# A two-layer decoder on one core: expert products computed transposed, expert weights fetched per tile, first weights of each stage awaited apart, two stages' inputs fetched ahead

## The chip, the cores and the metric

The kernel runs on one core of a Trainium2 chip. A core has five engines that run side by side and meet at semaphores: TensorE (PE, with its weight loads shown as PEld), VectorE (DVE), ScalarE (ACT), GpSimd (POOL) and SyncE (SP), which in this kernel issues most DMAs. All DMAs share 16 DMA engines. The metric is the device time of one execution in microseconds (us), lower is better. The median of three runs of the kernel before is 3891.22 us (3890.78 to 3893.25).

## The reference

The input x has 8 batches of 512 rows of 256 values, float32. Six sublayers follow each other, each with a residual sum and a layer norm:

```python
x = _layernorm(x + _L0_attn_ref(x, ...))     # 16 heads, scores times a decay table
x = _layernorm(x + _L0_xattn_ref(x, ctx, ctx, mask))   # keys and values are 64 context rows
x = _layernorm(x + _L0_ffn_ref(x, ...))      # 256 -> 1024, butterflies, gelu, butterflies, -> 256
x = _layernorm(x + _L1_attn_ref(x, ...))     # 16 heads of 64, rotary, causal
x = _layernorm(x + _L1_xattn_ref(x, ctx, ...))   # 8 heads over 512 + 64 keys
x = _layernorm(x + _L1_ffn_ref(x, gamma, beta, router_w, W1, W2))
```

The last one is a mixture of 8 experts, of which each row takes its best two:

```python
logits = jnp.einsum('btd,ed->bte', xn, router_w)
probs = jax.nn.softmax(logits / TEMP, axis=-1)
w, idx = jax.lax.top_k(probs, K)                       # K = 2
h = jax.nn.silu(jnp.einsum('btd,edf->betf', xn, W1))   # W1: 8 x 256 x 1024
y = jnp.einsum('betf,efd->betd', h, W2)                # W2: 8 x 1024 x 256
out = jnp.einsum('bte,betd->btd', wdense, y)           # and out + res
```

## The kernel before

x stays on the chip all the time, in `x_all`, 32 tiles of 128 rows. The sublayers run one after the other. Each is a function that opens a block: a written program for each engine, with semaphore waits placed by hand. A block ends when all five engines have ended, and the next one starts with all of them. So whatever an engine waits for at the head of a block stands alone on the clock. The loops over batches are unrolled, and within a block the order of the work on each engine is the order of the text.

- `load_block` (L268) fetches the identity matrix and all 4 MB of x, and ends when both have landed.
- `attention` (L446) serves three sublayers by its `kind`: `a0`, `a1` and `x1`. At its head SP issues the list `loads` (L713 to 732), and PE, DVE and SP wait for all of it at once (`wait_ge(weights, 16 * len(loads))`, L784, L1206, L1220). PE then starts the first batch from the list `START`: transpose x (`xT`, L803), the latent product (`lat`, L813; not in x1), the first queries and keys (`item`), and, in a1 and x1, the first values (`v`). In a0 GpSimd also writes zeros to the 33 MB area `moe_sent`, four MB ahead of each batch (L1157 to 1162).
- `cross_attention_heads` (the x0 stage, L1417) fetches the context twice over (`ctxT`, `vnat`), the head mask and the mask, waits for all, lets DVE build the values and the bias, and only then splits the context into two parts (ACT L1577, DVE L1663). GpSimd needs both parts for the keys (L1621), PE needs the keys for the scores (L1553).
- `fold_butterflies` (L1731) multiplies the butterfly stages into one up and one down matrix. SP issues `w_con`, `high`, the placed stages of the up side (`lowup`, 3.5 MB in two DMAs), four small ones and the down side. PE runs `rounds(0)` over `lowup` (L1793), then L1803, then `rounds(1)` over `lowdown`. DVE first folds the high stages of the down side (L1864, L1868), then those of the up side (L1877), the latter in turns with ACT (L1843).
- `route` (L2070) picks the experts of the last two batches, places the rows in `moe_sent` sorted by expert (GpSimd's indirect DMAs, L442), and SP fetches the weights of all experts, `w1` and `w2`, 8 MB each, in 16 DMAs (L2124, L2125). GpSimd ends with a wait for the last row to land.
- `experts` (L2277) runs 72 tiles of 128 sorted rows. Which expert a tile has is read from `expert_of` into a register. For a tile PE transposes the rows (`experts_X`, L2353), multiplies them with `w1` in two halves of 512 columns (`experts_H`, L2373: the rows are the loaded weights, `w1` streams through), and ACT applies silu (`experts_h`, L2406). Then come eight transposes back (`experts_HT`, L2386), copied out by DVE (L2432), and the product with `w2` (`experts_Y`, L2361), copied out by DVE (L2423) and stored by SP. PE's order for tile i is H(i), Y(i-1), X(i+1), HT(i). SP fetches the rows of tile i+2 once X(i) is done. An fp32 product is shown as two PE instructions per call, a transpose as one.
- `combine` (L2436) gathers the two results of each row, sums and normalises.

Of the kernel before, what the change touches and what calls it, by code (L numbers as in the profile page):

```python
# [39 lines left out]
CLEAR = 8 * P  # L40

# [226 lines left out]
def load_block(nc, sh, x, ident):  # L268

    with ExitStack() as ctx:  # L270
        env = Env(nc, ctx, "load")
        loaded = env.sem("loaded")
        block = ctx.enter_context(nc.Block())

        @block.sync
        def _(sp):
            sp.dma_start(sh.ident[:], ident).then_inc(loaded, 16)
            sp.dma_start(sh.x_all[:, :, :], x.rearrange("b (q p) d -> p (b q) d", p=P)).then_inc(loaded, 16)
            sp.wait_ge(loaded, 32)
# [166 lines left out]
def attention(nc, sh, kind, w, ro):  # L446
# [118 lines left out]
    with ExitStack() as ctx:  # L565
# [77 lines left out]
        weights = sem("weights")  # L643
        ready = sem("ready")
# [68 lines left out]
        loads = [(wo[:], tiled(w["w_o"]))]  # L713
        if a0:
            loads += [(wq[:], w["w_q"].rearrange("(t p) g c -> p t g c", p=P)),
                      (wkT[:], tiled(w["w_kT"])), (wvT[:], tiled(w["w_vT"])), (wdn[:], tiled(w["w_down"])),
                      (wupk[:], w["w_up_k"]), (wupv[:], w["w_up_v"]), (table[:], w["decay"]),
                      (halves[:], w["halves"])]
        if a1:
            loads += [(wq[:], tiled(w["w_q"])), (wdn[:], tiled(w["w_down"])),  # L720
                      (wupk[:], w["w_up_k"]),
                      (wupv[:], w["w_up_v"]), (table[:], w["causal"]), (cos[:], w["cos"]), (sin[:], w["sin"])]
        if x1:
            loads += [(wq[:], tiled(w["w_q"])), (wk1[:], tiled(w["w_k1"])), (wv1[:], tiled(w["w_v1"])),
                      (wk2[:], tiled(w["w_k2"])), (wv2[:], tiled(w["w_v2"])), (bo[:], w["b_o"].to_broadcast([P, D]))]
            loads += ro.loads(w)
        N_READY = {"a0": 4, "a1": 1, "x1": 6}[kind]

        @block.sync
        def _(sp):  # L730
            for to, src in loads:
                sp.dma_start(to, src).then_inc(weights, 16)
            if x1:
                sp.dma_start(ctxT[:], tiled(w["ctxT"][0])).then_inc(ctx_in, 16)

            def swap_halves(b, n):

                wait_apart(sp, (weights, 16 * len(loads)), (raw_done, b * 4 * G + n + 1), (sin_done, b * 4 * G + n + 1))
                for k in range(4):
                    sp.dma_start(raw_swapped[32 * k:32 * k + 32, n % 2, :],  # L740
                                 raw[32 * (k ^ 1):32 * (k ^ 1) + 32, n % 4, :]).then_inc(swapped[n % 2], 16)

            def spread_rows(b, k):

                wait_apart(sp, (weights, 16 * len(loads)), (turned, b * G + (k + 2)))
                g = k % G
                sp.dma_start(inv_dram[g % 2], inv_rows[:, g % 2, :]).then_inc(spilled, 16)
                wait_apart(sp, (weights, 16 * len(loads)), (spilled, b * 16 * G + 16 * (k + 1)))
# [32 lines left out]
        def _(pe):  # L781
            pe.sem_inc(t_full, T_CREDIT)
            pe.sem_inc(pv, 2)
            pe.wait_ge(weights, 16 * len(loads))  # L784
            if a0:

                pe.wait_ge(ready, 2)
# [94 lines left out]
            def finish(seg, turn, b, work):  # L882

                qt = work[1]

# [150 lines left out]
            def begin():  # L1036
                for work in START:
                    run(start, 0, 0, work)
# [116 lines left out]
        def _(pool):  # L1155
# [8 lines left out]
            if x1:  # L1164
                pool.wait_ge(ready, N_READY)
                pool.wait_ge(ro.cleared, 16 * (SLOTS // CLEAR))
# [10 lines left out]
            if a1:  # L1177
                pool.sem_inc(sin_done, 2)
                pool.sem_inc(low, LOW_GROUP)
                pool.wait_ge(ready, N_READY)  # L1180
# [22 lines left out]
        def _(dve):  # L1203

            if a0:
                dve.wait_ge(weights, 16 * len(loads))  # L1206
                nc.vector.memset(inv[:], 1.0).then_inc(ready, 1)
                nc.vector.tensor_tensor(wkT[:], wkT[:], wvT[:], ALU.add).then_inc(ready, 1)
                nc.vector.memset(v_sb[:], 0.0).then_inc(ready, 1)
# [3 lines left out]
            else:  # L1213
# [6 lines left out]
                dve.wait_ge(weights, 16 * len(loads))  # L1220
                if x1:
                    nc.vector.memset(ro.ones[:], 1.0).then_inc(ready, 1)
                    nc.vector.tensor_scalar(ro.first[:], ro.iota[:, 0:NE], float(AREA), None, ALU.mult).then_inc(ready, 1)
                    nc.vector.tensor_scalar(ro.upto[:, 0, :], ro.iota[:, 0:NE], float(AREA), None,
                                            ALU.mult).then_inc(ready, 1)
# [70 lines left out]
            def step(seg, turn, b, s, prev, own, nxt):  # L1296
# [7 lines left out]
                route = x1 and own and b >= 2  # L1304
                if route and s == 0:
# [95 lines left out]
            def begin():  # L1401
                for work in START:
                    if work[0] == "item":
                        low_parts(start, 0, 0, work[1], work[2])

# [9 lines left out]
def cross_attention_heads(nc, sh, w):  # L1415
# [15 lines left out]
    with ExitStack() as ctx:  # L1431
# [3 lines left out]
        ctxT = sb("ctxT", [P, DT, B, SC])  # L1435
        ctx_hl = sb("ctxhl", [P, 2, DT, B * SC], F32R)
        keys = sb("keys", [P, 2, DT, B, HH, SC], F32R)
        v_nat = sb("vnat", [P, B, D])
        v_all = sb("v", [P, B, PR * 2 * VC])
        hmask = sb("hmask", [P, HH])  # L1440
        mask = sb("mask", [P, B * QT, SC], I32)
# [13 lines left out]
        loaded = sem("loaded")  # L1455
# [52 lines left out]
        LOADS = DT + 2 + 2  # L1508

        @block.sync  # L1510
        def _(sp):
            for t in range(DT):
# [1114 lines left out]
```

## Time and profile before

| | us |
|---|---|
| median of three runs | 3891.22 |
| the profiled execution, its own time | 3911.24 |
| span of its instructions | 3909.4 |
| PE busy in the span | 3308.2 (85%) |
| PEld busy | 2437.9 (62%) |
| DVE busy | 2117.3 (54%) |
| ACT busy | 1919.8 (49%) |
| POOL busy | 972.7 (25%) |

The span is cut into 40 slices of 97.7 us. In the page's second part a digit is the busy share of a slice in tenths, PEclk is the granted clock of TensorE in tenths of full speed, and the last two rows are the share of the 16 DMA engines and GB/s:

```profile
PE   5888888858689589998899968999999939999970
PEclk9999999978899799999999989999999969999985
DMA  3111111010200222222222220000000051111113
```

PE is the busiest engine nearly everywhere. The dips are the borders of the stages: the start, slice 8 (a0 to x0), slice 10 (x0 to the fold), slice 13 (a1), slice 23 (x1), slice 32 (the routing), and the last 120 us, `combine`, where PE has no work. Times in rows are microseconds from the start of the span; a row of the timeline gives the start, the duration, the engine, line and operation, what is written and read, the number of instructions merged in it, and in brackets the idle time ahead of it and what ended that.

### The profile page before, as it was taken

To read this page: it belongs to the slowest core of one execution; us is meant where nothing else is said; L and a number is where in the kernel's file an instruction comes from. 1 tells how busy PE (TensorE), PEld (TensorE's weight loads), DVE (VectorE), ACT (ScalarE), POOL (GpSimd) and SP (SyncE) were. 2 spreads that over 40 slices of the span, in tenths; PEclk is the share of its full clock that TensorE was granted. 3 is DMA by queue.
4 is the path that set the end of the run, shared out by engine and by line. 5 is a ranking of instruction groups with operands and counts; after the bars stand their busy time and mean duration, and the time that the engine had idled before them with its cause. 6 is when DMAs were issued, how large, how long until landed. Compare 5 with 4: busy or idle time off the path is not lost. (4 is left out here: it accounts for less than half of the span.)

```text
span 3909.4 us, 73528 instructions
## 1 busy us (share of the span) xinstructions
PE 3308.2 (85%) x25632; PEld 2437.9 (62%) x25632; DVE 2117.3 (54%) x6935; ACT 1919.8 (49%) x4678; POOL 972.7 (25%) x790
## 2 busy tenths in 40 slices
PE   5888888858689589998899968999999939999970
PEld 3666566548678356666666656777777727677750
DVE  4777777756667345554555543566666642222226
ACT  4887788734432265555655544655555501111110
POOL 0000000026200376766677620001111130000014
PEclk9999999978899799999999989999999969999985
DMA  3111111010200222222222220000000051111113
GB/s 110 52 50 61 40 70 66 26 31 1 101 1 1 64 57 51 58 50 55 53 58 50 52 60 22 13 13 23 24 24 24 25 214 34 34 33 33 34 43 111
DMA packets 111253, 187.53 MB, mean 48 GB/s; under 512 B 23792, under 2 KB 66224, under 8 KB 106032
## 3 DMA queue, kind: packets, MB, share of 16 engines
q1 hardware_dynamic: 100000, 131.44, 11.8%
q0 software_dynamic: 10896, 51.39, 3.5%
q8 instruction: 216, 3.54, 0.4%
q14 instruction: 141, 1.16, 0.1%
HBM read 91.93 MB, written 57.28 MB: 38 GB/s over the span
## 5 line engine op out<-in xcount | busy, mean ns | idle before, releaser
L955 PE MATMUL a_T<-ident,a_t 128*128 128x128 f32 x3328 | 500.7, 284 | 89.1 <-ACT a_pT L1119 62.6
L955 PEld LDWEIGHTS a_T<-ident,a_t 128*128 128x128 f32 x3328 | 376.1, 144 | 285.4 <-issue 249.5
L1119 ACT ACTIVATE a_pT<-a_T 128x512 f32<-128x512 f32 (+3 forms) x768 | 368.4, 511 | 223.2 <-PE a_T L955 223.1
L1354 DVE CUSTOM_DVE_ANT_0 a_t<-a_A,a_decay 128x512 f32<-128x512 f32 x512 | 323.0, 687 | 102.5 <-PE a_A L920 102.2
L1132 ACT ACTIVATE a_t<-a_t,a_neg 128x512 f32<-128x512 f32 x512 | 362.7, 716 | 6.1 <-DVE a_neg L1365 4.9
L1359 DVE CUSTOM_DVE_ANT_0 a_t<-a_A,a_table 128x384 f32<-128x384 f32 (+3 forms) x512 | 221.2, 487 | 179.8 <-PE a_A L932 178.8
L1189 POOL TENSOR_TENSOR a_rsin<-a_rawswapped,a_sin 128x512 f32<-128x512 f32 x128 | 170.5, 1332 | 529.0 <-DMA a_rawswapped<-a_raw 445.9
L1132 ACT ACTIVATE a_t<-a_t,a_mx 128x384 f32<-128x384 f32 (+3 forms) x512 | 280.0, 551 | 0.0
L2423 DVE COPY experts_y<-experts_Y 128x256 f32<-128x256 f32 x72 | 30.6, 425 | 438.6 <-PE experts_Y L2361 438.6
L2373 PE MATMUL experts_H<-ex_w,experts_xgT 128*128 x576 | 261.4, 597 | 0.8 <-ACT experts_xgT L2400 0.6
L2361 PE MATMUL experts_Y<-ex_w,experts_hT 128*128 x1152 | 260.5, 379 | 1.0 <-DVE experts_hT L2432 1.0
L2361 PEld LDWEIGHTS experts_Y<-ex_w,experts_hT 128*128 128x128 f32 x1152 | 218.8, 190 | 61.3 <-issue 35.2
L1119 ACT ACTIVATE x_pT<-x_T 128x512 f32<-128x512 f32 (+1 forms) x320 | 177.0, 592 | 138.4 <-PE x_T L955 118.0
L1359 DVE CUSTOM_DVE_ANT_0 x_t<-x_A,x_table,x_mx 128x512 f32<-128x512 f32 x256 | 177.2, 748 | 122.2 <-PE x_A L932 121.7
L2464 POOL DMA_INDIRECT combine_got<-moe_results,moe_fetch x64 | 62.1, 970 | 627.0 <-PEq L2442 593.6
L1328 DVE COPY a_pT<-a_T 128x512 f32<-128x512 f32 (+3 forms) x256 | 148.2, 579 | 126.6 <-PE a_T L955 125.8
L2406 ACT ACTIVATE experts_h<-experts_H 128x512 f32<-128x512 f32 x144 | 86.0, 597 | 240.8 <-PE experts_H L2373 240.8
L1132 ACT ACTIVATE x_t<-x_t,x_mx 128x576 f32<-128x576 f32 x256 | 194.7, 765 | 0.0
L891 PE MATMUL a_A<-a_wo,a_oT 128*128 128x256 f32 x640 | 165.2, 411 | 32.7 <-DVE a_mx L1359 12.9
L976 PEld LDWEIGHTS a_O<-a_pT,a_v 128*64 128x64 f32 x2560 | 139.0, 138 | 67.9 <-ACT a_pT L1119 38.2
L932 PE MATMUL a_A<-a_khl,a_qhl 64*128 64x128 f32 (+3 forms) x1536 | 157.2, 336 | 25.2 <-POOL a_khl L1199 22.4
L1162 POOL DMA_DIRECT2D moe_sent<-a_zeros x33 | 17.5, 539 | 642.0 <-ACT a_xT L1088 642.0
(337 smaller groups left out, 6901.5 us busy)
## 6 DMA issues: line engine op xcount, KB each, us to landing
moe_sent<-a_zeros POOLq DMA_DIRECT2D x33, 1024.0 KB, 8.0
a_rawswapped<-a_raw SPq DMA_DIRECT2D x512, 64.0 KB, 2.0
a_invrep<-a_inv_dram SPq DMA_DIRECT2D x64, 256.0 KB, 4.0
ex_w<-in_f_w_dram SPq DMA_DIRECT2D x16, 1024.0 KB
experts_xg<-moe_sent SPq DMA_DIRECT2D x72, 128.0 KB, 2.0
moe_results<-experts_y SPq DMA_DIRECT2D x72, 128.0 KB, 1.7
x_invrep<-x_inv_dram SPq DMA_DIRECT2D x32, 256.0 KB
x_all<-in_x_dram SPq DMA_DIRECT2D x1, 4096.0 KB, 14.5
```

Of the source, the lines that this page charges most:

```text
L891: mm = pe.matmul(bank[:, 0:D], oT[:, t, qt * P:(qt + 1) * P], wo[:, t, :], start=(t == 0), stop=(t == n_o - 1))
L932: mm = pe.matmul(A[seg.bank(at)][:, 0:keys(u)], q_hl[r, gp, ql, j // 2, q], k_hl[r, gp, kl_, j // 2, 0:keys(u)], start=(n == 0), stop=(n = ...
L955: mm = pe.transpose(bank[:, kt, :], t_of(u, j, kt * P, (kt + 1) * P), sh.ident[:])
L976: mm = pe.matmul(O[pr][64 * half:64 * half + 64, q], v_sb[:, kt, col], p_tile(u, j, kt), start=(kt == 0), stop=last, skip_group_check=True)
L1119: nc.scalar.activation(to, of, ACT.Copy).then_inc(t_empty, 1)
L1132: nc.scalar.activation(t_of(u_e % U, j, 0, n), t_of(u_e % U, j, 0, n), ACT.Exp, bias=neg[:, slot, j:j + 1], scale=SCALE if a0 else -1.0, a ...
L1189: nc.gpsimd.tensor_tensor(rsin[:], raw_swapped[:, n % 2, :], sin[:], ALU.mult).then_inc(sin_done, 1)
L1328: nc.vector.tensor_copy(p_tile(u, 3, 0, kts), bank[:, 0:kts, :] if kts > 1 else bank[:, 0, :])\
L1354: nc.vector.tensor_tensor_reduce(t_of(s, j, 0, n), A[seg.bank(name)][:, 0:n], table[:, at:at + n], 1.0, LOWEST, ALU.mult, ALU.max, mx[:, s ...
L1359: nc.vector.tensor_tensor_reduce(t_of(s, j, 0, n), A[seg.bank(name)][:, 0:n], table[:, at:at + n], -SCALE, mx1[:, slot, j:j + 1] if x1 els ...
L2361: mm = pe.matmul(Y[parity][:], hT[:, f, :], w2[:, bass.ds(e, 1), f, :].rearrange("p a d -> p (a d)"), start=(f == 0), stop=(f == FT - 1))
L2373: mm = pe.matmul(H[half][:], xgT[:, dt, :], w1[:, bass.ds(e, 1), dt, half * 512:(half + 1) * 512] .rearrange("p a f -> p (a f)"), start=(d ...
```

## The change

It has four parts.

1. Experts. The inner values come out transposed: for each 128 of the 1024 columns, that block of `w1` is the loaded operand and the transposed rows stream through. So the back transposes, their DVE copies and the tile `h` are gone. SP fetches the `w1` of each tile by itself, 1 MB into one of two buffers, once H of the tile two before is done. `w2` stays resident and is fetched in `route`. PE's order for tile i is now H(i), X(i+1), Y(i-1).

```diff
@@ experts, SP
+            def weights_of(i, parity):
+                e = sp.value_load(expert_of[0:1, i:i + 1], min_val=0, max_val=NE - 1)
+                sp.dma_start(w1[:, parity], w1_dram[bass.ds(e, 1)].rearrange("a (t p) f -> p (a t) f", p=P))\
+                  .then_inc(w1_in[parity], 16)
+            for i in range(2):
+                sp.dma_start(xg[:, i, :], tile_rows(sp, i)).then_inc(xg_in[i], 16)
+                weights_of(i, i)
 step:
+                if i + 2 < TILES:
+                    sp.wait_ge(xt_full, i + 1)
+                    sp.dma_start(xg[:, parity, :], tile_rows(sp, i + 2)).then_inc(xg_in[parity], 16)
+                    sp.wait_ge(h_full, i * 2 + 2)
+                    weights_of(i + 2, parity)
                 if not first:
                     store(i - 1, 1 - parity)
@@ experts, PE
                 pe.wait_ge(xt_done, i + 1)
-                pe.wait_ge(h_act, i * 2 + 2)
+                pe.wait_ge(w1_in[parity], pair * 16 + 16)
                 for half in range(2):
-                    for dt in range(DT):
-                        mm = pe.matmul(H[half][:], xgT[:, dt, :],
-                                       w1[:, bass.ds(e, 1), dt, half * 512:(half + 1) * 512]
-                                       .rearrange("p a f -> p (a f)"), start=(dt == 0), stop=(dt == DT - 1))
+                    if i:
+                        pe.wait_ge(h_act, i * 2 - 1 + half)
+                    for j in range(FT // 2):
+                        f = half * (FT // 2) + j
+                        for dt in range(DT):
+                            mm = pe.matmul(H[half][:, j, :], w1[:, parity, dt, f * P:(f + 1) * P], xgT[:, dt, :],
+                                           start=(dt == 0), stop=(dt == DT - 1))
                     mm.then_inc(h_full, 1)
+                if more:
+                    transpose_rows(1 - parity, pair + (parity + 1))
+                if i == 1:
+                    pe.wait_ge(w_in, 16 * NE)
                 if not first:
                     down(i - 1, 1 - parity)
-                for half in range(2):
-                    pe.wait_ge(h_act, i * 2 + (half + 1 + 2))
-                    for j in range(FT // 2):
-                        f = half * (FT // 2) + j
-                        mm = pe.transpose(HT[half][:, j, :], h[:, f * P:(f + 1) * P], sh.ident[:])
-                    mm.then_inc(ht_full, 1)
@@ experts, ACT
+                if i >= 2:
+                    act.wait_ge(y_full, i - 1)
-                    nc.scalar.activation(h[:, half * 512:(half + 1) * 512], H[half][:], ACT.Silu).then_inc(h_act, 1)
+                    nc.scalar.activation(hT[:, parity, half * (FT // 2):(half + 1) * (FT // 2), :], H[half][:],
+                                         ACT.Silu).then_inc(h_act, 1)
@@ experts, DVE
-                for half in range(2):
-                    dve.wait_ge(ht_full, i * 2 + (half + 1))
-                    nc.vector.tensor_copy(hT[:, half * (FT // 2):(half + 1) * (FT // 2), :],
-                                          HT[half][:]).then_inc(ht_done, 1)
@@ route, SP
             for e in range(NE):
-                sp.dma_start(w1[:, e], w["w1"][e].rearrange("(t p) f -> p t f", p=P)).then_inc(w_in, 16)
                 sp.dma_start(w2[:, e], w["w2"][e].rearrange("(t p) d -> p t d", p=P)).then_inc(w_in, 16)
```

2. Attention. Each kind has two lists, `loads` with what is used first and `later` with the rest, on two semaphores. PE transposes x ahead of the wait for the first list.

```diff
         if a0:
+            loads = [(sh.ident[:], w["ident"]), (wkT[:], tiled(w["w_kT"])), (wvT[:], tiled(w["w_vT"])),
+                     (wdn[:], tiled(w["w_down"])), (halves[:], w["halves"]), early.x_batch(sh, w["x"], 0)]
+            later = [(wq[:], w["w_q"].rearrange("(t p) g c -> p t g c", p=P)), (wupk[:], w["w_up_k"]),
+                     (wupv[:], w["w_up_v"]), (table[:], w["decay"]), (wo[:], tiled(w["w_o"]))]
         if a1:
+            loads = [(wdn[:], tiled(w["w_down"])), (wq[:], tiled(w["w_q"])), (wupk[:], w["w_up_k"]),
+                     (cos[:], w["cos"]), (sin[:], w["sin"])]
+            later = [(wupv[:], w["w_up_v"]), (table[:], w["causal"]), (wo[:], tiled(w["w_o"]))]
         if x1:
+            loads = [(wq[:], tiled(w["w_q"])), (wk1[:], tiled(w["w_k1"])), (wk2[:], tiled(w["w_k2"])),
+                     (wv1[:], tiled(w["w_v1"])), (wv2[:], tiled(w["w_v2"]))]
+            later = [(wo[:], tiled(w["w_o"])), (bo[:], w["b_o"].to_broadcast([P, D]))] + ro.loads(w)
+        LOADED, MORE = 16 * len(loads), 16 * len(later)
@@ PE, begin
                 for work in START:
+                    if work == START[1]:
+                        pe.wait_ge(weights, LOADED)
+                    if work == (("item", 0, 0) if a0 else ("v", 0, 0)) and not x1:
+                        pe.wait_ge(more, MORE)
                     run(start, 0, 0, work)
```

DVE waits for `more` after its part of `START` (a0, a1) or at batch 1 (x1); PE in x1 at the first `y` of batch 1; GpSimd in x1 before its first scaling. In x1 `ctxT` of batch 0 is now issued ahead of both lists.

3. The start, and inputs fetched ahead. `load_block` is gone. A new object `Early` holds the buffers of the x0 stage's inputs and of `lowup`, and a0's SP issues, behind its two lists, x of batches 1 to 7, `ctxT`, both halves of `vnat`, the head mask, the mask and `lowup`: 15 DMAs on one semaphore. PE waits for it before the `xT` of batch 1.

```diff
+    LOADED = 16 * (B - 1 + DT + 2 + 2 + len(FOLD_GROUPS))
+            if a0:
+                early.load(sp, sh, w)
 project, xT:
+                    if a0 and b == 1:
+                        pe.wait_ge(early.loaded, early.LOADED)
@@ fold_butterflies, SP, behind w_con and high
-            for side in range(2):
-                for i, (a, z) in enumerate(GROUPS_OF):
...
+            sp.dma_start(up[:, 0], w["w_exp_b"].rearrange("(j p) d -> p j d", p=P)).then_inc(loaded_up, 16)
...
+            for i, (a, z) in enumerate(GROUPS_OF):
+                sp.dma_start(low[1][:, a:z], w["low"][1, :, a * FT:z * FT, :]
+                             .rearrange("p (s j) n -> p s j n", j=FT)).then_inc(staged[1][i][0], 16)
```

4. Order in x0. ACT's and DVE's split of the context comes first, then the split of x, and behind that DVE's memset and copies of the values and the bias. GpSimd waits for `ready` at 2 instead of 4, PE for 4 only before its first product with the values.

```diff
-            pool.wait_ge(ready, 4)
+            pool.wait_ge(ready, 2)
@@ DVE
             split_x(start, 0, 0)
+            nc.vector.memset(v_all[:], 0.0).then_inc(ready, 1)
+            dve.wait_ge(ready, 3)
...
+            nc.vector.tensor_scalar(bias[:], mask[:], 1.0e9, -1.0e9, ALU.mult, ALU.add).then_inc(ready, 1)
+            dve.wait_ge(ready, 4)
```

## Rows read from the trace of the kernel before

**Rows 1.** Stretch, length, busy PE, PEld, DVE, ACT, POOL (x instructions), clock, DMA share, GB/s
```profile
0.00:24.76 24.76, 0.00 (x0) 0.00 (x0) 0.00 (x1) 0.00 (x0) 2.01 (x5) 1.00 0.81 254
...
1301.60:1315.10 13.50, 0.00 (x0) 0.00 (x0) 0.11 (x1) 0.00 (x0) 0.00 (x0) 0.50 0.85 301
...
2334.40:2354.50 20.10, 1.95 (x9) 1.58 (x9) 1.74 (x6) 1.19 (x2) 0.00 (x0) 0.50 0.66 237
...
3209.50:3789.50 580.00, 578.14 (x2448) 404.39 (x2448) 124.45 (x216) 114.76 (x217) 0.00 (x0) 1.00 0.10 33
```

**Rows 2.** Timeline of the start of a0; last, DMA issues with time to landing
```profile
0.76 0.41 SPq L277 DMA_DIRECT2D ident<-in_ident_dram  x1
...
24.79 0.63 DVE L1208 TENSOR_TENSOR a_wkT<-a_wkT,a_wvT 128x512 f32<-128x512 f32 x1
...
35.24 2.91 PE L837 MATMUL a_A<-a_xT,a_wq 128*128 128x512 f32 x4
...
102.31 1.27 PE L803 MATMUL a_A<-ident,x_all 128*128 128x128 f32 x8
...
a_wq<-in_a_w_q_dram SPq DMA_DIRECT2D x1, 512.0 KB, 4.0
```

**Rows 3.** Timeline of the start of x0
```profile
824.55 1.87 DVE L1646 MEMSET x_v<- 128x2176 f32 x1 [1.11 <-PEq L565]
...
838.02 1.06 ACT L1577 ACTIVATE x_ctxhl<-x_ctxT 128x1024 fp32r<-128x1024 f32 x1 [34.60 <-DMA x_mask<-in_mask_dram]
...
840.83 1.29 DVE L1663 TENSOR_TENSOR x_ctxhl<-x_ctxT,x_ctxhl 128x512 fp32r<-128x512 f32 x2
...
842.20 4.04 POOL L1621 TENSOR_TENSOR x_keys<-x_ctxhl,x_hmask 128x512 fp32r<-128x512 f32 x4 [164.79 <-DVE x_ctxhl L1663]
...
848.00 0.69 DVE L1683 SCALAR_TENSOR_TENSOR x_t<-x_S,x_bias 128x512 f32<-128x512 f32 x1 [2.50 <-PE x_S L1553]
```

**Rows 4.** Timeline of the fold
```profile
1050.02 3.76 PE L1793 MATMUL fold_C<-fold_lowup 128*128 128x128 f32 x16 [19.16 <-DMA fold_lowup<-in_f_low_dram]
...
1059.55 3.25 DVE L1868 SCALAR_TENSOR_TENSOR fold_down<-fold_down,fold_high,fold_tmpdown 128x256 f32<-128x256 f32 x8
...
1072.00 3.26 DVE L1877 SCALAR_TENSOR_TENSOR fold_up<-fold_up,fold_high,fold_tmpup 128x257 f32<-128x257 f32 x8 [8.86 <-ACT fold_tmpup L1843]
```

**Rows 5.** Timeline of the first product behind the weights in a1 and in x1
```profile
1317.77 3.78 PE L813 MATMUL a_A<-a_xT,a_wdn 128*128 128x512 f32 x4 [0.69 <-ACT a_xT L1088]
...
2354.49 5.52 PE L847 MATMUL x_A<-x_xT,x_wq 128*128 128x512 f32 x8 [0.69 <-ACT x_xT L1088]
```

**Rows 6.** The end of the routing: a stretch, the timeline, and one DMA's landing
```profile
3180.00:3200.00 20.00, 0.00 (x0) 0.00 (x0) 8.55 (x29) 0.00 (x0) 14.89 (x15) 0.50 1.05 395
...
3198.36 0.97 POOL L442 DMA_INDIRECT moe_sent<-moe_router,moe_place  x1 [0.30 <-issue]
3207.43 0.37 SPq L2323 DMA_DIRECT2D experts_xg<-moe_sent  x1
...
fold_down<-in_f_w_con_dram SPq DMA_DIRECT2D x1, 1024.0 KB, 5.4
```

**Rows 7.** Timeline of PE in one tile of the experts, and the last product
```profile
3504.61 1.04 PE L2386 MATMUL experts_HT<-ident,experts_h 128*128 128x128 f32 x8
3505.48 3.60 PE L2373 MATMUL experts_H<-ex_w,experts_xgT 128*128 x8
3508.92 3.62 PE L2361 MATMUL experts_Y<-ex_w,experts_hT 128*128 x16
...
3785.79 3.72 PE L2361 MATMUL experts_Y<-ex_w,experts_hT 128*128 x16 [1.03 <-DVE experts_hT L2432]
```

**Rows 8.** Fold products of the coming shape: timeline, one line's instructions (ns), groups
```profile
1068.05 1.95 PE L1793 MATMUL fold_C<-fold_lowdown 128*128 128x128 f32 x16
...
L1793 PEld LDWEIGHTS fold_C<-fold_lowdown x16: 188/192/192, 1067.8 to 1069.6; 128*128 128x128 f32 x16
...
L1793 PE MATMUL fold_C<-fold_chainup,fold_lowup 128*128 128x128 f32 x80 | 9.9, 285 | 0.0
```

More of the change, by code:

```diff
@@ L783, in _ @@
             pe.sem_inc(pv, 2)
-            pe.wait_ge(weights, 16 * len(loads))
             if a0:
-                pe.wait_ge(ready, 2)
+                pe.wait_ge(weights, LOADED)
+                pe.wait_ge(ready, 3)
                 for dt in range(DT):
@@ L1304, in step @@
                 route = x1 and own and b >= 2
+                if x1 and b == 1 and s == 0:
+                    dve.wait_ge(more, MORE)
+                    nc.vector.tensor_scalar(ro.first[:], ro.iota[:, 0:NE], float(AREA), None, ALU.mult).then_inc(ready, 1)
+                    nc.vector.tensor_scalar(ro.upto[:, 0, :], ro.iota[:, 0:NE], float(AREA), None,
+                                            ALU.mult).then_inc(ready, 1)
+                if route and b == 2 and s == 0:
+                    dve.wait_ge(ready, N_READY + 2)
                 if route and s == 0:
@@ L1645, in _ @@
         def _(dve):
-            nc.vector.memset(v_all[:], 0.0).then_inc(ready, 1)
             dve.sem_inc(s_read, 2 * DT)
@@ L1726, in fold_butterflies @@
         sb, sem = env.sb, env.sem
-        low = [sb(f"low{side}", [P, LOW, FT, P]) for side in ("up", "down")]
+        low = [early.low_up, sb("lowdown", [P, LOW, FT, P])]
         chain = [sb(f"chain{side}", [P, 2, FT, P]) for side in ("up", "down")]
@@ L1738, in fold_butterflies @@
         T = [env.ps(f"T{i}", [P, S]) for i in range(2)]
-        GROUPS_OF = ((0, 3), (3, 7))
-        staged = [[sem(f"staged_{side}{i}") for i in range(2)] for side in ("up", "down")]
+        GROUPS_OF = FOLD_GROUPS
+        staged = [[(early.loaded, early.LOADED)] * 2, [(sem(f"staged_down{i}"), 16) for i in range(2)]]
         loaded_up = sem("loaded_up")
@@ L2514, in decoder @@
         sh = Shared(nc, ctx)
-        load_block(nc, sh, w["x"], w["ident"])
         ro = Routing(nc, ctx)
-        attention(nc, sh, "a0", part("a0_", decay=w["decay"], halves=w["halves"]), ro)
-        cross_attention_heads(nc, sh, {n: w[n] for n in ("ctx", "ctxT", "mask", "head_mask8")})
-        butterfly_ffn(nc, sh, part("f0_"))
+        with ExitStack() as first_layer:
+            early = Early(nc, first_layer)
+            attention(nc, sh, "a0", part("a0_") | {n: w[n] for n in ("x", "ident", "decay", "halves", "ctx", "ctxT", "mask",
+                                                                    "head_mask8")} | {"low": w["f0_low"]}, ro, early)
+            cross_attention_heads(nc, sh, early)
+            butterfly_ffn(nc, sh, part("f0_"), early)
         attention(nc, sh, "a1", part("a1_", causal=w["causal"], cos=w["cos"], sin=w["sin"]), ro)
```

179 lines of the change are left out of this document (79 added, 100 removed).

## The prediction

> **What bounds the kernel now.** I read these views. First the page's slices, for where the dips are, then the busy times by stretch [rows 1], cut at those dips. The reader is to see two kinds of stretch. In the experts PE is busy 578.1 of 580.0 us at the full clock (1.00, so 2.4 GHz), DVE 124 and ACT 115, the DMA engines 0.10 busy: PE alone bounds them. At the borders PE does next to nothing while the DMA engines are 0.66 to 0.85 busy: 24.8 us at the start, 13.5 us ahead of a1, 20.1 us ahead of x1. There a landing bounds, and since a stage starts only when the one before has ended, each of these microseconds is on the path. Second, the timeline at these borders [rows 2 to 6], for the first instruction that works and what released it. Third, the timeline within one tile [rows 7] and of the one place where PE already runs the shape that the experts are to have [rows 8].
>
> **The sum is made against the profiled execution:** 3911.2 us (span 3909.4 and 1.8 around it), which lies 20.0 us above the median of 3891.2. I take the gain over to the median as it is.
>
> **Part 1a, the tile of the experts.** Starts of PE's groups in one tile [rows 7]: HT at 3504.61, H at 3505.48, Y at 3508.92. So eight transposes take 0.87 us and the eight instructions of H 3.44 us; 16 of Y and two of X make 3.66, and the period is 7.97 us. (A row's duration is 0.16 to 0.18 longer than the step to the next start; the end overlaps.)
> - Removed: HT, 0.87 us. The DVE copies (1.3 us a tile) were beside PE and give nothing, but for the last tile.
> - Changed: H becomes 2 halves x 4 blocks x 2 x 2 = 32 instructions of 128 columns, each with a weight load. The fold runs just that, fp32, 128x128 loaded, 128 columns streamed [rows 8]: 16 in 1.95 us, each 0.275 long, so (1.95 - 0.275) / 15 = 0.112 us apart. The loads are 0.192 long and yet the pitch is 0.112: they overlap. H is 32 x 0.112 = 3.57 us, 0.13 more than now. The cost could be up to 9.9 / 80 = 0.124 each [rows 8], a group that holds waits for ACT's copies: 3.96 us, 0.52 more. I take 0.112, the row without a wait in it.
> - Period after: 7.97 - 0.87 + 0.13 = 7.23; times 72: 53 us. Bounds: (0.87 - 0.52) x 72 = 25, and 0.87 x 72 = 63 if H stayed at 3.44.
> - The last product waits 1.03 us for DVE's copy [rows 7]; that goes: 1 us. Sum 54 us.
> - New waits. ACT's for y_full(i-1) and PE's for h_act are met a product earlier. PE's for `w1_in` is the one that matters. SP issues the fetch for tile i+2 when H(i) ends, about 1.2 us later (a wait, a register read as before each row fetch, the issue). Until H(i+2) PE has two periods less one H, 14.46 - 3.57 = 10.9 us, so the landing may take 9.7 us. A 1 MB fetch took 5.4 us from issue [rows 6]: hidden with 4 us to spare, at a need of 1.3 MB per 7.23 us = 181 GB/s where the routing drew 395 [rows 6]. Behind SP's wait for h_full stand that fetch and the store of Y(i-1), which isn't computed by then; nobody is late for it.
>
> **Part 1b, the routing.** The DMA engines are full (share 1.05 at 395 GB/s) to the end [rows 6], and the block ends with them. 8.4 MB less is 21 us of that queue, but GpSimd's last send is issued at 3198.36 + 0.97 = 3199.3, at its own pitch of 0.97 + 0.30 = 1.27; with 2 us of landing (the first row fetch, issued at 3207.43, had its transposes at 3209.5 [rows 1, 6]) and the block's border SP's first row fetch comes at about 3202.6 instead of 3207.43: 4.8 us. What is late next is the first `w1`: issued 1.2 us behind the first row fetch (3203.8), landed 5.4 later, H(0) at 3209.3; before, the first transposes stood at the cut of 3209.5 [rows 1] and H(0) 1.2 later. Left: 1.4 us (-2 to +4).
>
> **Part 2 and 3, the start.** Work began at 24.79 [rows 2]. Now six DMAs are issued from 0.76 on [rows 2], about 0.5 apart, the last (x of batch 0, 512 KB) at 3.25; 512 KB behind another load took 4.0 us [rows 2]. DVE begins at 7.2: 17.6 us (16.5 to 18.5). Second wait: the first product with `wq` stood at 35.24, so now at 17.6; `later` is 1.4 MB more, at the 254 GB/s of the start [rows 1] 5.5 us, landed by 13. Covered by 4 us. The 15 early DMAs are 10 MB, and 4 MB of zeros come between: 56 us at that rate, so about 69, and PE's wait before the `xT` of batch 1 stands at 102.31 - 17.6 = 84.7 [rows 2]. SP may be stuck issuing until then, with the first spread of the softmax sums behind it; DVE reads those only shortly ahead of that `xT`. No cost; without this cover it would be the microseconds past 84.
>
> **x0.** Now the block starts at 824.5, ACT's copy follows the mask's landing at 838.02, DVE's part ends at 842.1, the keys at 846.24, the first scores reach DVE at 848.00 [rows 3]. After: ACT 824.5 to 825.6, DVE 1.29 to 826.9, GpSimd 4.04 to 831.0, scores 1.8 later: 832.8. DVE in the meantime: the split of x, two subtractions like those of L1663, 1.3; memset 1.87; copies and bias, which fill it from 838.02 to 840.83, 2.8: 826.9 + 6.0 = 832.9. The two meet, so 848.0 - 833.0 = 15.0 us (14 to 15.5).
>
> **The fold.** PE waits until 1050.02 for `lowup` [rows 4]; it can start at 1040.5 with the block, 9.5 us. But DVE has the down side until 1059.55 + 3.25 = 1062.8, 0.4 for the bias, and starts on the up side at 1063.2 instead of 1072.00 [rows 4]: 8.8 us, and that chain of DVE and ACT in turns ends the fold. ACT's share is ready at 1062.5. SP's queue is 3.5 MB shorter, so `lowdown` lands ahead of its use. 8.8 us (6 to 9.5).
>
> **a1 and x1.** PE's first product behind the weights stood at 1317.77 and 2354.49 [rows 5]. In a1 301 GB/s over 13.5 us are 4.06 MB [rows 1]; with the same 2 us for the first byte that is 353 GB/s. The first list is 2.25 MB: 1301.6 + 2 + 6.4 = 1310.0, so 7.8 us (7 to 9). In x1 the first list with `ctxT` is 2.7 MB: 2334.4 + 2 + 7.6 = 2344.0, so 10.5 us (9 to 11). The transposes of x run beside the landing in both. The second lists land within 5 us, a1's ahead of the first values (10 us later), x1's a batch ahead.
>
> **Sum:** 54 + 1.4 + 17.6 + 15.0 + 8.8 + 7.8 + 10.5 = 115 us. 3911.2 - 115 = 3796.2 for the profiled execution; as a median 3891.2 - 115 = 3776.
>
> **Rivals.**
> - Part of it is eaten (slower pitch or a second list late): H at 0.124 gives 25 instead of 53, and the lower bounds of the borders take another 10. 115 - 28 - 10 = 77: 3814. For it: the x80 row. Against: the same row holds waits, and the one without is 0.112.
> - Slower: the weight loads don't hide. If each of the 32 costs its 0.192 us [rows 8], H is 6.14, a tile 1.83 longer (6.14 - 3.44 - 0.87), 132 us in all against 62 gained elsewhere: 3891 + 70 = 3961. It decides from the pitch at which a tile loses 62 / 72 = 0.86: H at 5.17, 0.162 each. For it: the row's load durations, and twice as many instructions in the tile. Against: the same row's pitch.
>  The Trainium skill speaks for it ("TensorE: Matmul & The Clock Gate", Back-to-back issue gap): it puts sustained products of 128 columns at 81 ns and of 512 at 131 ns, so short ones cost much more per column. By that, as an estimate, a tile would go from 8 x 131 + 8 x 81 to 32 x 81 ns, 0.9 us more, and the kernel would end 3 us above before. In this trace H's 512 columns are 0.43 apart and the fold's 128 are 0.112, nearly a quarter: the measurement decides.
> - Slower: the fetch bounds. With two buffers two periods are landing + 1.2 + 3.57; slower than before from a period of 8.83, a landing of 12.9 us. Say 13.5: 9.13, 1.16 x 72 = 84 lost against 62: 3913. For it: 1 MB behind other loads. Against: 5.4 us by itself, and two tiles' row traffic is small.
> - The starts don't move (a stage's first work waits for something that I don't see): only the experts' 54: 3837. For it: I infer the releasers. Against: each stood next to a landing.
>
> **How the numbers follow.** Forecast 0.80, eaten 0.10, starts unmoved 0.05, weight loads 0.02, fetch 0.02, and 0.01 for no change. This kernel's runs tell 0.2% (8 us) from nothing. Faster by more 0.95, same 0.01, slower 0.04. The range: the upper bound of the gains is 63 + 4 + 1 + 18.5 + 15.5 + 9.5 + 9 + 11 = 131, which all at once is unlikely, so I start at 3763; at the other end 3802, two thirds of the way to the eaten case, which leaves some 2 in 10 outside, unmoved starts among them.
>
> **What would show it.** After: H's groups 3.6 apart from the next, no HT, period 7.23; DVE's first work at 7, the x0 scores at 15 us less behind the border, PE in the fold within 1 us of its start, PE busy with `lat` 8.5 us into a1. Wrong if PE idles before H on `w1_in`, if H's pitch is above 0.12, or if DMA waits for `more` or the early loads show on PE.

## The result, and the profile after

| | before | after |
|---|---|---|
| median, us | 3891.0 (3878.5 to 3893.3, 4 runs) | 3795.1 (3790.6 to 3800.3, 4 runs) |
| ratio after / before | | 0.976 [0.9736, 0.9785] |
| the profiled execution, its span | 3909.4 | 3792.5 |
| last PE product of the experts to the end | 120.3 | 102.1 |

The kernel became 96 us faster; 115 were forecast, and the measured median lies inside the forecast range (3763 to 3802). The profiled execution came out at 3794.4 us against 3796.2 forecast, but that agreement is partly luck: 18 of its 117 us against the profiled execution of before are the last line of the table, which no step of the forecast touches (below). Up to the last product of the experts the two traces are 98.8 us apart (3789.12 against 3690.36).

The busy times by stretch, at the cuts that answer to [rows 1], and the last stage:

```profile
0.00:7.70 7.70, 0.00 (x0) 0.00 (x0) 1.88 (x2) 0.00 (x0) 2.01 (x5) 1.00 0.67 191
1271.70:1280.10 8.40, 0.00 (x0) 0.01 (x1) 0.11 (x1) 0.00 (x0) 0.00 (x0) 0.50 0.82 309
2300.60:2311.30 10.70, 0.00 (x0) 0.00 (x0) 1.62 (x4) 0.00 (x0) 0.00 (x0) 0.50 0.89 299
3165.60:3690.80 525.20, 524.37 (x3598) 494.06 (x3598) 30.16 (x71) 105.49 (x215) 0.00 (x0) 1.00 0.52 178
3690.80:3792.50 101.70, 0.00 (x0) 0.00 (x0) 69.01 (x258) 0.00 (x0) 62.72 (x64) 0.51 0.42 125
```

The gaps without PE work shrank from 24.8 to 7.7 us at the start, from 13.5 to 8.4 ahead of a1, and from 17.4 to 10.8 ahead of x1 (2334.43 to 2351.87 before; the 20.1 of [rows 1] held PE's transposes too). In the experts PE is still busy all the time, DVE does 30 us instead of 124, and the DMA engines are 0.52 busy at 178 GB/s (181 were forecast as the need). The timeline of PE in two tiles, beside [rows 7]:

```profile
3299.90 3.62 PE L2387 MATMUL experts_Y<-ex_w,experts_hT 128*128 x16
3303.35 3.73 PE L2401 MATMUL experts_H<-experts_xgT,experts_w 128*128 128x128 f32 x32
3306.92 0.38 PE L2379 MATMUL experts_X<-ident,experts_xg 128*128 128x128 f32 x2
3307.14 2.11 PE L2387 MATMUL experts_Y<-ex_w,experts_hT 128*128 x9
```

From Y to the next Y are 7.24 us, from the start of H to the next group 3.57, which is 32 x 0.112. There is no idle time in it, and no HT. The first H is another matter; the experts' first two groups of PE and the landing before them:

```profile
3161.54 0.69 PE L2379 MATMUL experts_X<-ident,experts_xg 128*128 128x128 f32 x2 [32.53 <-DMA experts_xg<-moe_sent]
...
3165.62 6.25 PE L2401 MATMUL experts_H<-experts_xgT,experts_w 128*128 128x128 f32 x32 [3.40 <-DMA experts_w<-in_f_w_dram]
```

It waits 3.40 us for `w1` and then takes 6.25 us instead of 3.6: the granted clock is 0.50 (1.2 GHz) until 3170.8, behind 37 us in which PE did nothing but two transposes. That is no loss to the kernel before, whose first H (8 instructions, 3.60 us long elsewhere) was slow as well:

```profile
3210.73 5.77 PE L2373 MATMUL experts_H<-ex_w,experts_xgT 128*128 x8 [0.56 <-ACT experts_xgT L2400]
```

The heads of the stages, beside [rows 2 to 5]. Timeline: the first DVE work of a0, the first read of the scores in x0, the first product of the fold; then PE at the head of a1 and of x1 (L833 transposes x; L843 and L877 are the first products behind the weights):

```profile
7.73 0.69 DVE L1247 TENSOR_TENSOR a_wkT<-a_wkT,a_wvT 128x512 f32<-128x512 f32 x1 [4.63 <-DMA x_all<-in_x_dram]
...
813.94 1.06 ACT L1606 ACTIVATE x_ctxhl<-early_ctxT 128x1024 fp32r<-128x1024 f32 x1 [20.60 <-PEq L588]
...
823.31 1.29 DVE L1700 SCALAR_TENSOR_TENSOR x_t<-x_S,x_bias 128x512 f32<-128x512 f32 x2
...
1018.60 0.41 SPq L1787 DMA_DIRECT2D fold_down<-in_f_w_con_dram  x1
1018.80 3.75 PE L1815 MATMUL fold_C<-early_lowup 128*128 128x128 f32 x16 [9.66 <-PEq L1475]
...
1271.77 0.38 SPq L758 DMA_DIRECT2D a_wdn<-in_a_w_down_dram  x1
...
1280.13 1.94 PE L833 MATMUL a_A<-ident,x_all 128*128 128x128 f32 x8 [16.33 <-DVEq L1262]
...
2311.39 1.94 PE L833 MATMUL x_A<-ident,x_all 128*128 128x128 f32 x8 [19.06 <-DVEq L1262]
...
2314.01 5.38 PE L877 MATMUL x_A<-x_xT,x_wq 128*128 128x512 f32 x8 [0.69 <-ACT x_xT L1124]
```

The reader is to see one thing that should not be there. The transposes of x in a1 and x1 (L833) start 8.4 and 10.8 us behind the stage's first DMA issue, not at once. PE's own wait for the weights stands behind them; what released them is DVE's queue at L1262. There DVE waits for the first list, and only then gives the credits `a_dve` that let PE write its first bank (a bank is a buffer that PE writes its results into; a credit says that it is free).

### The profile page after: what moved, and what is told of

Same layout as the page of the kernel before. It is cut to its first block and busy times, and to the rows that moved or that the text cites. A ratio compares the mean times of both kernels' runs of the same rounds, so it can differ in the third digit from the quotient of the medians.

```text
span 3792.5 us, 75673 instructions
## 1 busy us (share of the span) xinstructions
PE 3267.4 (86%) x26784; PEld 2538.5 (67%) x26784; DVE 2024.4 (53%) x6791; ACT 1912.7 (50%) x4678; POOL 972.8 (26%) x790
## 5 line engine op out<-in xcount | busy, mean ns | idle before, releaser
L2428 ACT ACTIVATE experts_hT<-experts_H 128x512 f32<-128x512 f32 x144 | 86.0, 597 | 415.0 <-PE experts_H L2401 415.0
L2401 PEld LDWEIGHTS experts_H<-experts_xgT,experts_w 128*128 128x128 f32 x2304 | 270.9, 193 | 8.4 <-issue 3.8
L2401 PE MATMUL experts_H<-experts_xgT,experts_w 128*128 128x128 f32 x2304 | 271.5, 277 | 4.1 <-DMA experts_w<-in_f_w_dram 3.4
L1198 POOL DMA_DIRECT2D moe_sent<-a_zeros x33 | 17.6, 539 | 647.1 <-ACT a_xT L1124 647.1
## 6 DMA issues: line engine op xcount, KB each, us to landing
ex_w<-in_f_w_dram SPq DMA_DIRECT2D x8, 1024.0 KB, 12.9
```

Source lines behind the costliest of these rows:

```text
L2401: mm = pe.matmul(H[half][:, j, :], w1[:, parity, dt, f * P:(f + 1) * P], xgT[:, dt, :], start=(dt == 0), stop=(dt == DT - 1))
L2428: nc.scalar.activation(hT[:, parity, half * (FT // 2):(half + 1) * (FT // 2), :], H[half][:], ACT.Silu).then_inc(h_act, 1)
```

## The experiments

Ratios and leads are against runs of the kernel before on the same chip. Runs e1 to e4 shared one chip, and so did e5 to e8, and e9 to e12.

**e1, the kernel before a second time.**

> The kernel before, unchanged, for a second trace. Theory (the first profiled execution was disturbed once): its last stage, combine, took 119.9 us from the last PE product to the end, against 101.8 in the kernel after, and 10 us of it are idle DVE waits that name no releaser of this core. If that was a one-off, combine is 101 to 103 us here and the span some 18 us shorter, about 3890. Rival (combine is shorter because the change made it so): 119 to 121 us again, span about 3909.

Measured: 3902.4 us, span 3900.6. The stretch behind the experts by busy time, first in this trace, then in the first trace of before:

```profile
3798.60:3900.50 101.90, 0.00 (x0) 0.00 (x0) 68.93 (x258) 0.00 (x0) 62.89 (x64) 0.51 0.42 125
```

```profile
3789.50:3909.00 119.50, 0.00 (x1) 0.00 (x0) 69.94 (x258) 0.00 (x0) 62.10 (x64) 0.51 0.36 107
```

The same 258 DVE instructions, 69 to 70 us of work, in 102 or 120 us. So the shorter `combine` is not the change's, and the rival is out. But the long form isn't a one-off either, as the theory had it. Every trace of e1 to e4 and of e9 to e12 has 101.9 to 102.7 us, every one of e5 to e8 122.2 to 123.5, and the median of before was 3914 us beside these four, 3895.5 and 3897 beside the others. The span did not fall to 3890 as expected: up to the last product this execution was 9.1 us longer than the first one (3798.20 against 3789.12).

**e2, part 1 alone** (`moe`, `route` and `experts` of after in the kernel before), and **e3, parts 2 to 4 alone** (the reverse).

> The kernel before with part 1 alone (transposed inner values, w1 per tile, order H, X, Y, the routing fetches only w2). Theory, by the trace of after: 72 periods of 7.24 instead of 7.98 us are 53 us, the last wait 1, the routing end 1.7: 55 us, so about 3836 against 3891 (ratio 0.986). Rival (the experts gave more in the median than the periods say, or the parts disturb each other): below 3825 or above 3845.

> The kernel after with the experts and the routing of before: parts 2, 3 and 4 alone. Theory: 43 us, the lead of the kernel after at the end of x1 in the trace, so about 3848 (ratio 0.989). Rival (the borders give their forecast 60 us and the loss to it was chance in one trace): about 3831.

Measured (leads by the ratio): e2 3835.6 us, 0.9854 [0.9834, 0.9873], 57 us; from the first H to the last product 524.8 us against 578.3 in e1. e3 3840.6 us, 0.9857 [0.9842, 0.9873], 56 us; 578.8 us from the first H to the last product, so nothing of the experts' gain comes from elsewhere. e2's theory holds. e3's lead (49 to 62 us by its interval) is above the 43 of its theory and reaches the rival's 60; the steps at the heads of the stages, 51 us (next section), lie inside. The 43 is not the lead that the traces show at the end of x1: the routing's first DVE instruction stands at 3151.79 us before and at 3105.41 after, 46.4 apart. And that place scatters, 3160.85 in e1 (the kernel before) and 3097.97 in e3.

**e4, credits ahead of the wait.**

```diff
+                dve.sem_inc(a_dve, A_BANKS)
                 dve.wait_ge(weights, LOADED)
                 dve.wait_ge(ready, N_READY)
-            dve.sem_inc(a_dve, A_BANKS)
+            if a0:
+                dve.sem_inc(a_dve, A_BANKS)
```

> The kernel after, in which DVE gives its bank credits (a_dve) ahead of its wait for the first weights in a1 and x1. Theory: PE's transposes of x stand behind these credits, not behind PE's own wait, so they now start within 1 us of the stage's start and the first product behind the weights comes 2.6 us earlier in each of a1 and x1: 5 us less than after in all. Rival (something else of the landing holds the transposes): they stay 8.3 and 10.7 us behind the stage's start, and the time is that of after.

Measured: 3784.4 us, 0.9722 [0.9707, 0.9737]. The heads of a1 and x1, timeline (SP issues its first DMA at 1265.00 and at 2290.54):

```profile
1265.50 1.94 PE L833 MATMUL a_A<-ident,x_all 128*128 128x128 f32 x8 [8.48 <-DVE a_inv L1253]
1273.68 3.75 PE L843 MATMUL a_A<-a_xT,a_wdn 128*128 128x512 f32 x4 [6.24 <-issue]
...
2292.51 1.97 PE L833 MATMUL x_A<-ident,x_all 128*128 128x128 f32 x8 [10.28 <-DVE moe_ones L1259]
2300.57 5.29 PE L877 MATMUL x_A<-x_xT,x_wq 128*128 128x512 f32 x8 [6.09 <-issue]
```

The transposes start 0.5 us into a1, as expected, and 2.0 us into x1, where DVE gives its credits only behind four memsets. From the first issue to the first product behind the weights are 8.68 us instead of 10.98 in a1; in x1, from the issue of `wq`, 9.56 instead of 12.91. That is 2.3 and 3.35, 5.7 together: the credits held the transposes, and the rival is out. In a1 a part is lost again: PE's first eight instructions behind the weights all run at a granted clock of 0.50 here (6.1 us), in after only the first four, and the first product with `wupk` (L859) is 15.2 us behind the first issue instead of 16.4, which leaves 1.2 of the 2.3. In x1 the first product with `wk` keeps the gain (15.2 instead of 18.6 us behind the first issue). The distance to after's own ratios (0.976, 0.9764 and 0.9747, in other comparisons) is 10 to 16 us, more than these steps explain.

**e5, the kernel after again.**

> The kernel after, unchanged. Its first four runs gave 96 us less than before; the two halves alone gave 57 and 56, 112 in all, and the credits variant 108. Theory (the steps seen in the traces are all there is: start 17.0, x0 14.0, fold 8.9, a1 5.2, x1 6.7, routing 1.7, experts 53.7, together 107; the rest is how PE's clock happens to fall in the attention stages, a few us a run either way): 0.973, about 104 us less. Rival (in the whole kernel the parts cost each other some 15 us): 0.976 again.

Measured: 3815.6 us against 3914.3, 0.9764 [0.9746, 0.9781], 92 us by the ratio and 99 by the medians. The theory's 0.973 is just outside the interval; the rival's 0.976 came.

**e6, PE kept at work ahead of the first products** (on top of e4).

```diff
+                    if work == START[1]:
+                        for _ in range({"a0": 0, "a1": 3, "x1": 5}[kind]):
+                            pe.matmul(O[1][:], sh.ident[:], sh.x_all[:, 0:2, :], start=True, stop=True)
...
+            warm(5)
             transpose_rows(0, 1)
+            warm(8)
```

> The credits variant, in which PE also runs products whose results nobody reads, so that it does not stand idle ahead of the first real ones: 3 of 512 columns behind the transposes of x in a1, 5 in x1, and in the experts 5 of 128 columns ahead of the first rows and 8 ahead of the first H. Theory (PE's clock is at 0.5 in the first microseconds of work after a wait, and comes up only with work: the first four instructions of lat took 0.86 us each instead of 0.43, the first H 6.25 instead of 3.6): lat and the first products of x1 at 0.43, 1.8 us each, the first H 2.5 us shorter: 6 us less than the credits variant, 0.9706. Rival (the clock goes by something that these products do not change, or they delay the real ones): the first H stays at 6.2 us, time as the credits variant or up to 5 us more.

Measured: 3801.7 us against 3914.3, 0.971 [0.9691, 0.9729], and 14 us under e5 on the same chip. Timeline of PE: a1, x1 and the first tiles (L1072 and L2418 are the idle products).

```profile
1272.22 5.28 PE L1072 MATMUL a_O<-x_all,ident 128*128 128x512 f32 x6 [0.69 <-ACT a_xT L1126]
1277.40 1.98 PE L843 MATMUL a_A<-a_xT,a_wdn 128*128 128x512 f32 x4
...
2292.45 7.17 PE L1072 MATMUL x_O<-x_all,ident 128*128 128x512 f32 x10 [0.69 <-ACT x_xT L1126]
2299.46 3.60 PE L877 MATMUL x_A<-x_xT,x_wq 128*128 128x512 f32 x8
...
3151.63 3.31 PE L2418 MATMUL experts_Y<-ident 128*128 128x128 f32 x16
3155.34 3.81 PE L2405 MATMUL experts_H<-experts_xgT,experts_w 128*128 128x128 f32 x32 [0.40 <-DMA experts_w<-in_f_w_dram]
```

`lat` takes 1.98 us where e4 had 3.75, the eight instructions with `wq` 3.60 instead of 5.29 (5.38 in after), the first H 3.81 instead of 6.55 (6.25 in after). So the first real products run at full clock in all three places, as the theory had it, but that is not yet the gain. In x1 the ten idle instructions outlast the wait: the first with `wq` stands 11.6 us behind the stage's first issue, against 10.0 in e4, and the first with `wk` 15.1 against 15.2. Nothing is gained there; the rival's delay ate it. In a1 the first product with `wupk` comes 11.9 us behind the first issue instead of 15.2, 3.4 gained, and the experts take 2.8 us less from the first H to the last product. The sum is the 6 of the theory, from two places instead of three. Against e5 the same three places give 10 of the 14 us (4.6, 3.3 and 2.3).

**e7 and e8, `w1` fetched twice and three times.**

```diff
-                sp.dma_start(w1[:, parity], w1_dram[bass.ds(e, 1)]...).then_inc(w1_in[parity], 16)
+                for to in [w1] + idle:
+                    sp.dma_start(to[:, parity], w1_dram[bass.ds(e, 1)]...).then_inc(w1_in[parity], 16)
```

> The kernel after, in which SP fetches each tile's w1 twice, the second time into a buffer that nobody reads; PE waits for both. Theory (the fetch has slack: it may land 9.7 us after its issue and takes 5.0; two would take about 7.7 at the 395 GB/s of the routing, and 2.4 MB per 7.24 us are 326 GB/s): period 7.24, time as after within 4 us. Rival (the fetch is close to bounding, so its 5.0 us are not the price that counts behind row traffic): a period of 7.6 or more, 26 us or more lost.

> The same with three fetches of each tile's w1, two of them into buffers that nobody reads. Theory: 3.41 MB per tile at 395 GB/s are 8.6 us, so the DMA engines bound and the period is 8.6 to 8.8: 100 to 112 us more than after, about 3900. Rival (landing, not the rate, bounds: three landings in a row, 10.3 us, plus 1.2 and 3.6 over two periods): a period of 7.6, 26 us more.

Measured: e7 3812.3 us, 0.9752 [0.9732, 0.9773], e8 3914.0 us, 1.0007 [0.9987, 1.0027]; e5 on the same chip 3815.6. The same 300 us of the experts by busy time, in e7 and then in e8; the third fence is e8's timeline of PE at two tiles:

```profile
3300.00:3600.00 300.00, 300.00 (x2078) 283.07 (x2078) 17.41 (x41) 60.93 (x125) 0.00 (x0) 1.00 0.89 328
```

```profile
3300.00:3600.00 300.00, 267.19 (x1780) 241.38 (x1780) 15.28 (x36) 51.99 (x106) 0.00 (x0) 0.99 1.02 405
```

```profile
3399.73 0.38 PE L2381 MATMUL experts_X<-ident,experts_xg 128*128 128x128 f32 x2
...
3408.03 0.38 PE L2381 MATMUL experts_X<-ident,experts_xg 128*128 128x128 f32 x2
```

With two fetches PE is busy 300 of 300 us; the DMA engines are 0.89 busy. With three they are full (1.02) at 405 GB/s and the tile takes 8.30 us, a little less than the theory's 8.6 to 8.8; e8 is 98 us above e5, where 100 to 112 were expected. The rival's period of 7.6 is out. It took the landing as a fixed price, and it is none: the median from issue to landing is 5.0 us for the one fetch of after, 7.6 for the second of e7 and 10.1 over the two extra ones of e8. So the rate bounds, as the theory had it, and the fetch of the change has room for twice its bytes.

**e9, e10, e11, the whole and its halves on one chip.**

> The kernel after once more, beside its two halves on one chip. So far it was 96 and 99 us ahead (two chips), its halves 57 and 56 on a third. Theory (the parts add; the steps of the traces come to 107): the lead here equals the sum of the two halves' leads within 8 us. Rival (in the whole kernel the parts cost each other some 15 us): the lead stays 15 us below that sum again.

> Part 1 alone, on the same chip. Both theories: 55 us by its steps (0.986). What counts is the sum with the other half.

> Parts 2 to 4 alone, on the same chip. Both theories: 52 us by its steps (17.0, 14.0, 8.9, 5.2, 6.7), 0.987. What counts is the sum with the other half.

Measured, against 3897.1: e9 3794.4 us, 0.9747 [0.9729, 0.9765]; e10 3836.3 us, 0.9838 [0.9818, 0.9859]; e11 3842.9 us, 0.9869 [0.9852, 0.9887]. The halves multiply to 0.9709, the whole is 0.0038 above, 15 us (12 by the medians). The three half-widths (0.0018, 0.0021, 0.0018) add in quadrature to 0.0033, 13 us. So the rival, 15 us short, is at the value; parts that add exactly are just outside the interval, parts that add within the theory's 8 us are not. No step in the traces shows the 15 us (next section), so what makes them stays open.

**e12, two more steps on e6.** In x1 the five idle products ahead of the weights also make room for two behind the first queries.

```diff
+                    if work == START[1] and x1:
+                        pe.wait_ge(folded, 16)          # only wq counts here
@@ experts, SP
             for i in range(2):
+                weights_of(i, i)
                 sp.dma_start(xg[:, i, :], tile_rows(sp, i)).then_inc(xg_in[i], 16)
-                weights_of(i, i)
```

> The warm variant with two more steps: SP issues each of the first two w1 fetches ahead of the rows of its tile, and in x1 PE waits for wq alone ahead of the first queries, on a semaphore of its own, and for the rest of the first list behind them. Theory (the first H waits for w1, which is issued 1.2 us behind the rows; in x1 the first queries stand behind the landing of the whole list): first H 1.2 us earlier, x1 2 to 3 us, so 4 us less than the warm variant, 12 to 16 us less than after. Rival (the rows land later and hold the first H, and behind the queries PE waits for the same last landing): as the warm variant.

Measured: 3773.0 us against 3897.1, 0.9692 [0.9671, 0.9713], 21 us under e9 on the same chip. It has the lowest ratio here, but e6's interval (0.9691 to 0.9729) overlaps its own, so it is not shown to be faster than e6. Of its two steps one works. In x1 the products with `wk` start 12.3 us behind the issue of `wq`, against 14.6 in e6: 2.3 us. The other loses. SP and PE at the head of the experts, timeline:

```profile
3147.66 0.40 SPq L2353 DMA_DIRECT2D experts_w<-in_f_w_dram  x1
...
3148.87 0.35 SPq L2358 DMA_DIRECT2D experts_xg<-moe_sent  x1
...
3153.05 0.69 PE L2389 MATMUL experts_X<-ident,experts_xg 128*128 128x128 f32 x2 [3.88 <-DMA experts_xg<-moe_sent]
3153.53 3.62 PE L2424 MATMUL experts_Y<-ident 128*128 128x128 f32 x16
```

The 128 KB of rows, issued 1.2 us behind 1 MB of weights, had their transposes 4.2 us after the issue instead of 2.1 ([rows 6], [rows 1]: issued 3207.43, used 3209.5), and the eight idle products then stood ahead of H for another 3.6. The first H starts 9.3 us behind SP's first issue, against 6.3 in e6. The second H starts 3.8 us later behind the routing than in e6. For that step the rival was right and dearer than it said, and both steps together cost 1.5 us.

## Why the prediction was right in kind and 19 us too large a gain

By its own steps, from the traces of before and after. A step runs from the stage's first instruction to the one that the prediction named, in x0 from the first that is no DMA issue (824.55 and 813.94).

| step | forecast | measured |
|---|---|---|
| start of a0: first DVE work, first PE product | 17.6 | 17.0 (25.56 to 8.56) |
| x0: start of the stage to the first read of scores | 15.0 | 14.1 (23.4 to 9.4) |
| fold and ffn: first issue to a1's first issue | 8.8 | 8.1 (261.3 to 253.2) |
| a1: first issue to `lat` | 7.8 | 5.2 (16.2 to 11.0) |
| x1: first issue to the first queries | 10.5 | 6.7 (20.1 to 13.4) |
| routing's last PE products (a row of two, its start) to the first H | 1.4 | 0.2 (37.5 to 37.3) |
| first H to the last product | 54 | 53.7 (578.4 to 524.7) |
| sum | 115 | 105 |

- **The tile** was right to a hundredth: 7.24 against 7.23 us, by the pitch of 0.112 us that the fold showed. The fold's row had just the shape that was coming. The 9.9 / 80 of the same view, taken as the upper bound, contained waits and would have halved the gain. By the estimate that the prediction worked out from the Trainium skill's figures ("TensorE: Matmul & The Clock Gate", Back-to-back issue gap), this kernel would have ended 3 us above before; the trace disagrees: 32 short fp32 instructions take 3.57 us where 8 long ones took 3.44. The weight loads do hide: 494 us of them beside 524 of products.
- **The fetch** was hidden with the room that was claimed (e7: twice the bytes at the same period). The rival was priced by a landing of 12.9 us and a period of 8.83; e8 shows another bound ahead of it, full DMA engines at a period of 8.30.
- **The step that failed is in a1 and x1**: "The transposes of x run beside the landing in both." They did not. Two engines had to be let go, and the diff lets go only one: DVE still gives PE's bank credits behind its own wait for the weights. At the first product this is 5.7 us (e4: 2.3 and 3.35) of the 6.4 that the two steps came short. It could be read ahead of time. The reader of a removed wait must ask for each semaphore that the freed instructions wait for, credits among them, who gives it and what that engine waits for. The landing of a1's list was forecast right (8.4 us into the stage); in x1 the first list came 10.8 us into it, not 9.6, and that is the rest of the shortfall.
- **x0 and the fold**: DVE's prelude in x0 ended at 823.3, its own work 1 us longer than summed (the split of x, the memset and the copies run from 816.3 to 823.3, 7.0 instead of 6.0). The scores were there first, so DVE is what bounds that head now.
- **The routing** came 1.2 us short by the step of the table. Behind the last PE products SP's first row fetch came 3.1 us earlier (34.2 to 31.1), not 4.8: from the end of GpSimd's last send to that fetch are 4.9 us (3154.54 to 3159.45), where the forecast had 2 for the landing and 1.3 for the border, and no row showed the 1.3. The first H then waited for `w1`, as named, 0.5 us less than forecast. The table's step also leaves out a loss in front of it. From the routing's first DVE instruction to its last PE products are 21.5 us in both traces of before and 22.6 to 23.0 in all twelve others. The router's products, before and after:

```profile
3163.87 3.94 PE L2140 MATMUL route_R<-route_router,route_xnT 128*128 128x8 f32 x32
```

```profile
3117.92 6.83 PE L2160 MATMUL route_R<-route_router,route_xnT 128*128 128x8 f32 x32
```

  They run at a granted clock of 0.92 and of 0.50; 1.8 us come back in a DVE conversion behind them (2.01 before, 0.18 after). Why the clock is up there only in the kernel before stays open: the idle time ahead is the same 16.6 us in e2, which is slow too. So from its first DVE instruction to the first H the routing did not become 1.4 us shorter but 1.3 longer (58.9 to 60.2).
- **From 105 to 96.** The forecast carried the gain from the profiled execution to the median as it was. That was sound: of the 20 us by which the profiled execution stood above the median, 18 were `combine`, which no step touches (e1). At the last product of the experts the two traces are 98.8 us apart, 6 less than the steps. Between the steps the lead changed by -6.4 us in a0 (17.0 to 10.6), -3.0 in x0, -1.2 in a1, +5.9 in x1 and -1.5 in the routing's head, and only the last comes back in every trace. In a0 4.7 of it were lost in the first batch, where PE's instructions of 512 columns stood 0.86 us apart and those of before 0.43. But that batch takes 81.4 us in this trace of after and 76.5 and 76.9 in e5 and e9, the same kernel, and 76.8 and 78.8 in the two traces of before; over all traces a0 from its first product to the stage's end takes 799 to 810 us with the old start (4 traces) and 798 to 806 with the new (10). So this isn't the early loads' doing; it scatters. A single trace does not settle a few us here: the profiled executions of e5 and e9 lay 10 us under their own medians. By medians, the lead of the whole was 96, 99 and 103 us in three comparisons, the sum of the halves 115 in two, the sum of steps 105. Why the whole lies below its halves was not settled.

The rivals: none came. The nearest was "eaten", by another mechanism than the one named (not the pitch, but a wait that remained in force).

## What to carry to other kernels

Take the price of a new instruction stream from a place in the same trace that already runs its exact shape without waits: that gave 53.7 of 54 us here. When a wait is moved behind some work, follow that work's other semaphores, the buffer credits too, back to engines that still wait at the old place. Measure a step from the start of its stage: behind a later event a loss ahead of it, as in the routing, goes unseen. And where two executions of one kernel differ by more than the effect of a step, compare stage by stage up to a common instruction before any difference is given to the change.

## What the runs showed of the hardware

- `combine` has two lengths on identical code: 102 us beside two groups of runs, 122 to 123 beside the third, and 120 once in the first profiled execution of before, with 69 to 70 us of DVE work in both. In the long form DVE stands still 1 to 3 us between instructions of its own chain. The waits in the trace of e5, behind the experts (engine, tile, releaser, total, times, longest):

```profile
DVE combine_scratch L184 <- DVE combine_scratch L181: 3.4, 5, 1.6
DVE combine_scratch L168 <- remote: 3.1, 1, 3.1
...
DVE combine_mv L150 <- remote: 2.9, 1, 2.9
```

  What DVE waits for there the trace does not show.
- At the heads of a1, x1 and the experts PE's first products run at a granted clock of 0.50, behind 16 to 37 us with next to no PE work (6.25 us for an H of 3.6). Products without any use, run in the wait, buy 3.4 us back in a1 and 2.8 at the first H, and nothing in x1, where they outlast the wait (e6 against e4).
- One core's DMA engines moved 405 GB/s with a share of 1.02 (e8). 128 KB issued behind 1 MB had their user 4.2 us later, alone 2.1 (e12).
